# Attention unit of a gated four-layer block: the fourth exponent block joins the partial sum by an accumulating DMA, and the PE sums columns once

## The reference, cut to what matters

```python
def _L1_xattn_ref(q, k, v):
    qh = q.reshape(b * h, d // h, m)          # b 16, h 8 heads, d // h 32, m 512
    kh = k.reshape(b * h, d // h, -1)
    vh = v.reshape(b * h, c // h, -1)
    qk = jnp.einsum('bdm,bdn->bmn', qh, kh) * scale
    sm = jax.nn.softmax(qk, axis=-1)
    ret = jnp.einsum('bmn,bcn->bcm', sm, vh)
    return ret.reshape(b, c, m)
x = x + jnp.tanh(g_xattn[1]) * _L1_xattn_ref(_layernorm(x, axis=-1), ctx_2048, ctx_2048)
```

## Time and profile before

| what | value |
|---|---|
| median of three runs | 1845.89 us (1845.26 to 1846.24) |
| profiled execution | 1844.25 us |
| its span, first to last instruction | 1842.5 us |
| mean granted PE clock | 0.950 of full speed |
| PE busy over the span | 1619.3 us, 88% |
| POOL busy over the span | 850.0 us, 46% |
| attention: first `part_sum` addition to the last | 676.91 us to 1155.94 us |

### The profile page before, as it was taken

One profiled execution on the slowest core, in us unless ns is written; L12 is line 12 of the kernel. 1 busy time (PEld: TensorE's weight loads), 2 busy tenths in 40 slices (PEclk: granted clock), 3 DMA queues, 4 the chain that ended last, 5 costly groups with the idle time before them and its releaser, 6 DMA issues. The chain is left out here.

```text
span 1842.5 us, 24658 instructions
## 1 busy us (share of the span) xinstructions
PE 1619.3 (88%) x6946; PEld 881.0 (48%) x6946; DVE 995.2 (54%) x1724; ACT 660.5 (36%) x1211; POOL 850.0 (46%) x760
## 2 busy tenths in 40 slices
PE   4688888887767279999999999786999999999997
PEld 3566666665533034444444443245444444444443
DVE  6488888888636367777777774275111111111111
ACT  7311111112624536777777777320111111111111
POOL 0344444443304637888888888203333333333332
PEclk9999999998878669999999999887999999999999
DMA  6333333334735785666666661740333333333333
GB/s 184 99 125 125 125 126 127 126 126 108 192 73 213 274 183 133 156 156 155 155 155 155 155 155 53 261 150 24 61 68 68 69 69 69 69 69 69 69 69 46
DMA packets 110369, 223.95 MB, mean 122 GB/s; under 512 B 12256, under 2 KB 12256, under 8 KB 109408
## 3 DMA queue, kind: packets, MB, share of 16 engines
q1 hardware_dynamic: 85696, 169.10, 33.4%
q0 software_dynamic: 15904, 37.23, 11.6%
q10 hardware_dynamic: 8704, 16.78, 2.4%
HBM read 146.71 MB, written 75.84 MB: 121 GB/s over the span
## 5 line engine op out<-in xcount | busy, mean ns | idle before, releaser
L1362 DVE TENSOR_REDUCE low<-pA 128x2 f32<-128x1024 f32 x256 | 307.5, 1224 | 143.3 <-PE pA L1198 132.4
L400 PE MATMUL y<-kv,toep 128*128 128x288 f32 x1280 | 329.2, 413 | 47.7 <-DVEq L63 36.6
L1328 ACT ACTIVATE pt<-pB 128x512 f32<-128x512 f32 x512 | 286.9, 593 | 125.0 <-PE pB L1216 119.2
L400 PEld LDWEIGHTS y<-kv,toep 128*128 128x128 f32 x1280 | 239.3, 191 | 137.6 <-DVEq L63 64.8
L1774 POOL DMA_INDIRECT out_rows<-XN,slots x71 | 112.6, 1587 | 356.7 <-DVE XN L1757 356.7
L1700 PE MATMUL pH<-WF,XN 128*128 x568 | 257.2, 596 | 1.1 <-DVE XN L1748 0.9
L1715 PE MATMUL pY<-WP,XN 128*128 x568 | 255.6, 593 | 0.8 <-ACT XN L1741 0.8
L1216 PE MATMUL pB<-qs,ks 98*128 98x512 f32 x512 | 227.0, 447 | 2.9 <-ACT pt L1328 2.4
L357 POOL TENSOR_TENSOR kv<-kc 128x2048 f32<-128x2048 f32 x32 | 115.2, 3600 | 243.0 <-DMA kc<-in_ctx_conv 177.5
L1198 PE MATMUL pA<-ks,qs 96*128 96x512 f32 x512 | 189.0, 414 | 36.0 <-DMA qs<-q_low 34.4
L1748 DVE COPY XN<-p9T 128x512 f32<-128x512 f32 x71 | 49.1, 692 | 258.4 <-PE p9T L1692 258.4
(11 more groups left out here) (241 smaller groups left out, 1951.7 us busy)
## 6 DMA issues: line engine op xcount, KB each, us to landing
ks<-ctx_high SPq DMA_DIRECT2D x64, 256.0 KB, 4.7
qs<-q_high SPq DMA_DIRECT2D x64, 256.0 KB, 6.2
kc<-in_ctx_conv SPq DMA_DIRECT2D x32, 384.0 KB, 5.8
XN<-in_x SPq DMA_DIRECT2D x16, 512.0 KB, 4.2
ct<-in_ctx SPq DMA_DIRECT2D x16, 512.0 KB, 4.8
toep<-kernel_and_skip SPq DMA_DIRECT2D x32, 256.0 KB, 4.2
ctx_high<-kh ACTq DMA_DIRECT2D x16, 512.0 KB, 5.3
ctx_low<-kl ACTq DMA_DIRECT2D x16, 512.0 KB, 7.0
```

Of the source, the lines that this page charges most:

```text
L400: m = pe.matmul(y[half].rearrange("p (l n) c -> p l n c", l=CB)[:, l, :, 0:PAIRS], toep[u][:, (l - s) * P:(l - s + 1) * P], kv[u][:, half, ...
L1328: act.activation(pt[s][:, h, :], bank(u, n), ACT.Exp, scale=SCALE1).then_inc(s_exp, 1)
L1362: dve.tensor_reduce(ap(low[u % 2], t % CB * NH + t // CB, [[NH, 2], [1, 1]]), pA[n % 2], op=ALU.max, axis=AX.X, negate=True).then_inc(s_re ...
```

## The change

The fourth block of exponents no longer goes to PE for its column sums. POOL issues two transfers from SBUF to SBUF, each adding half of `pt[3]` (128 rows of 4 KB) to the same half of `part_sum`, and PE then sums `part_sum` alone. `part_sum` has two buffers, chosen by the parity of the unit. Each POOL addition now waits for its own half of the exponents. The blocks on PE move: `values` s = 0 to beat 15 of the unit, s = 1, 2, 3 to beats 2, 5, 7 of the next, the one `sums` to its beat 11. The logarithm moves to after the exponent of beat 12, the inverse to after that of beat 14, `scale` to beat 15.

```diff
-        part_sum = sb(st, "part_sum", [P, NH, C])
+        part_sum = [sb(st, f"part_sum{i}", [P, NH, C]) for i in range(2)]
+        s_acc = [sem(f"s_acc6{i}", st) for i in range(2)]
+        def landed(eng, j, i, u):
+            eng.wait_ge(s_acc[u % 2], 32 * (TRIP // 2 * i + u // 2) + 32)
             def body(j, i, u):                     # POOL
-                pool.wait_ge(s_exp, made(j, place(j, 1, NH - 1)))
-                wait(pool, s_sum, 2 * j - 1)
+                mine = part_sum[u % 2]
+                wait(pool, s_sum, j - 1)
                 for n in range(2):
+                    pool.wait_ge(s_exp, made(j, place(j, 1, 2 * n + 1)))
-                    pool.tensor_tensor(part_sum[:, 2 * n:2 * n + 2], pt[0][...], pt[1][...], ALU.add)
+                    pool.tensor_tensor(mine[:, 2 * n:2 * n + 2], pt[0][...], pt[1][...], ALU.add)
...
+                for n in range(2):
+                    pool.wait_ge(s_exp, made(j, place(j, CB - 1, 2 * n + 1)))
+                    pool.sem_inc(s_go, 1)
+                    pool.dma_start(mine[:, 2 * n:2 * n + 2], pt[CB - 1][:, 2 * n:2 * n + 2], accum_op=ALU.add).then_inc(s_acc[u % 2], 16)
                 if exists(j - 1):
                     add_row(j - 1)
...
-            def sums(j, u, last):                  # PE: two calls, beats 5 and 7
+            def sums(j, i, u):                     # PE: one call, beat 11
+                landed(pe, j, i, u)
+                wait(pe, s_att, j)
                 for h in range(NH):
-                    m = pe.matmul(pO[...], ones, rows[:, h, :], start=not last, stop=last)
+                    m = pe.matmul(pO[...], ones, part_sum[u % 2][:, h, :], start=True, stop=True)
             def finish(j, i, u, beat):
                 if beat == 2:
+                    values(j, i, u, 1)
+                if beat == 5:
                     values(j, i, u, 2)
-                if beat == 5:
-                    sums(j, u, False)
                 if beat == 7:
-                    sums(j, u, True)
-                if beat == 10:
                     values(j, i, u, 3)
+                if beat == 11:
+                    sums(j, i, u)
...
-                    if beat == 13:
+                    if beat == 15:
                         values(j, i, u, 0)
-                    if beat == 15:
-                        values(j, i, u, 1)
...
-                    else:                          # ACT, before exponent block 3
-                        wait(act, s_sum, 2 * j)
+                    elif exists(j - 1):
+                        landed(act, *following(j, i, u, -1))
```

More of the change, by code:

```diff
@@ L1162, in body @@
                     halves(j + 1, (u + 1) % TRIP)
-                pool.wait_ge(s_exp, made(j, place(j, 1, NH - 1)))
-                wait(pool, s_sum, 2 * j - 1)
+                mine = part_sum[u % 2]
+                wait(pool, s_sum, j - 1)
                 for n in range(2):
-                    pool.tensor_tensor(part_sum[:, 2 * n:2 * n + 2], pt[0][:, 2 * n:2 * n + 2], pt[1][:, 2 * n:2 * n + 2],
+                    pool.wait_ge(s_exp, made(j, place(j, 1, 2 * n + 1)))
+                    pool.tensor_tensor(mine[:, 2 * n:2 * n + 2], pt[0][:, 2 * n:2 * n + 2], pt[1][:, 2 * n:2 * n + 2],
                                        ALU.add).then_inc(s_add, 1)
                     pool.wait_ge(s_add, 4 * j + n + 1)
-                pool.wait_ge(s_exp, made(j, place(j, 2, NH - 1)))
                 for n in range(2):
-                    pool.tensor_tensor(part_sum[:, 2 * n:2 * n + 2], part_sum[:, 2 * n:2 * n + 2], pt[2][:, 2 * n:2 * n + 2],
+                    pool.wait_ge(s_exp, made(j, place(j, 2, 2 * n + 1)))
+                    pool.tensor_tensor(mine[:, 2 * n:2 * n + 2], mine[:, 2 * n:2 * n + 2], pt[2][:, 2 * n:2 * n + 2],
                                        ALU.add).then_inc(s_add, 1)
                     pool.wait_ge(s_add, 4 * j + n + 3)
+                for n in range(2):
+                    pool.wait_ge(s_exp, made(j, place(j, CB - 1, 2 * n + 1)))
+                    pool.sem_inc(s_go, 1)
+                    pool.dma_start(mine[:, 2 * n:2 * n + 2], pt[CB - 1][:, 2 * n:2 * n + 2], accum_op=ALU.add).then_inc(s_acc[u % 2], 16)
                 if exists(j - 1):
@@ L1228, in values @@
                 m.then_inc(s_av, 1)
-            def sums(j, u, last):
-                if last:
-                    pe.wait_ge(s_exp, made(j, place(j, CB - 1, NH - 1)))
-                else:
-                    pe.wait_ge(s_add, 4 * j + 4)
-                    wait(pe, s_att, j)
-                rows = pt[CB - 1] if last else part_sum
+            def sums(j, i, u):
+                landed(pe, j, i, u)
+                wait(pe, s_att, j)
                 for h in range(NH):
-                    m = pe.matmul(pO[(u + 1) % 2][h * HD1:(h + 1) * HD1, :], ones, rows[:, h, :], start=not last, stop=last)
+                    m = pe.matmul(pO[(u + 1) % 2][h * HD1:(h + 1) * HD1, :], ones, part_sum[u % 2][:, h, :], start=True, stop=True)
                 m.then_inc(s_sum, 1)
@@ L1293, in logarithm @@
             def logarithm(j, u):
-                act.wait_ge(s_sum, 2 * j + 2)
+                act.wait_ge(s_sum, j + 1)
                 wait(act, s_inv, j)
@@ L1336, in body @@
                             keep(j + 1, bank(u, TURN), made(j, TURN))
-                        if NH * s + h == TURN and exists(j - 1):
+                        if NH * s + h == TURN + 2 and exists(j - 1):
                             logarithm(j - 1, u - 1)
-                        if NH * s + h == TURN + 2 and exists(j - 1):
+                        if NH * s + h == TURN + 4 and exists(j - 1):
                             inverse(j - 1)
@@ L1384, in body @@
                         measure(j - 2, (u + 2) % TRIP)
-                    if beat == 13 and exists(j - 1):
+                    if beat == 15 and exists(j - 1):
                         scale(j - 1, u - 1)
```

## The result

The changed kernel takes 1936.31 us (median of 4 runs, 1935.43 to 1937.16) against 1846.07 us for the kernel before on the same chip: ratio 1.0488, 95% interval 1.0469 to 1.0506, so 90 us slower. The prediction said slower, 1903 us with 1846 to 1950 as its range. The sign and the first cause held. The size was short by 33 us, and lies outside the 1877 to 1928 that the prediction gave for its own mechanism. The profile shows why: a late landing and a falling clock took part, which the prediction had counted at nothing and at 2%.

The account below looks back on a forecast made before the run. PE paced the attention before; POOL, with two 1.5 us transfers, would set 17.1 us units. Attention +52.4 and stage end +5.3 give +57.7 on 1844.25, 1902, forecast as 1903 us against the median; range 1846 to 1950.

Parts of the forecast that it names:

- its own mechanism: Attention: POOL as the bound, one transfer costing 1.07 to 1.9 us; 1877 to 1928 us, taken at 1903, chance 67%.
- POOL becomes the bound: Attention unit: two transfers at 1.5 us each on POOL's 14.1 us of work make a unit 17.1 us.
- The rival of a nearly free issue: POOL's two issues: under 0.5 us per transfer, so PE sets the unit; 1822 or 1814 us, chance 14%.
- PE would fall to 14.0 us: PE's attention unit: one sums block fewer takes 1.19 us off 15.18, with DVE and ACT not becoming the bound.
- A late landing costs nothing: PE's wait at `sums`: a late landing costs up to 0.4 us, covered by PE's 3.1 us to spare.
- signs of being wrong: Profile: cheap POOL issues with PE at 100%, `sums` and exponent block 3 waiting for landing, or granted clock under 1.00.
- the engine-bound rival: Transfer engines: adding 4 KB rows takes twice the scatter's time, making units 19.0 us; 1960 us, chance 10%.
- The rival of a falling clock: PE's clock halves because PE idles 3 of 17 us; a unit is 28 us, +400 us, chance 2%.
- The first units: First three attention units: without `add_row` or `refine` in part, 13.4 to 14.8 us of POOL work each, 43.6 together.
- The end of the stage: After the last additions: PE waits 6.3 us for the landing and saves one block, 1.0; +5.3 us.
- The cover for POOL's new wait: POOL's wait for exponent block 3 before issuing: exponents are done 1.7 us before its additions end, so no cost.
- The draw: POOL's issues: with SP's 0.48 us per transfer a unit is 15.06 us; 1846 us in all, chance 7%.

## Why the prediction was right, and where it fell short

*POOL becomes the bound.* Right, and shown twice: against the kernel without transfers, 46 us are lost with two one-column transfers and 92 with four. POOL's floor is 16.76 us against 17.1 forecast. One transfer was taken as 1.5 us with its gap; two are 1.79 us together, with a single gap of 0.65 ahead of them, 2.44 in all and inside its bounds of 2.1 to 3.8. From the last addition to the end of `add_row` are 3.76 us where they were 1.47; that and wider gaps between the additions (0.16 us for 0.08) put the floor 16.76 - 14.1 = 2.65 us above the work that POOL had before, instead of 3.0. The rival of a nearly free issue is out. The Trainium skill (DMA: Bandwidth & Descriptors, Anatomy of one DMA — SWDGE path) calls descriptor generation small; this case's trace does not agree, with a row of 0.89 us of busy POOL for 128 rows.

*PE would fall to 14.0 us.* Wrong, and hidden behind the first point. That step divided PE's order into blocks and matmuls and let neither DVE nor ACT become the bound because each has some 11 us of work in a unit. Both reach PE through two buffers only, so they hold it up over a few beats, though not over the unit. Without transfers the unit is 15.48 us in the new order, 15.13 in the old, 14.5 with half the reductions. The last shows it for DVE; for ACT it is read from PE's waits and no run isolates it. The rivals that ended at 1822 and 1814 us could not have come about at all: the best that this order allowed, with a free fourth block, was 1853.

*A late landing costs nothing.* This is the step that made the forecast 33 us short. It took 4.8 to 7.1 us for the landing; it is 9.8. It let PE's slack pay, 3.1 us; the slack was 16.76 - 15.48 = 1.3. And it gave no price to the half clock that followed many of these waits, but to a fallen clock of the whole stage, at 2%. Of the 37 us between one-column and full transfers (1936.3 - 1899.5), the later loads give back 30 and busy work in the idle stretch 20, so they overlap and do not add up.

*The signs and the range.* Of the signs of being wrong that the prediction listed, two came, `sums` waiting for the landing and a granted clock under 1.00. With one-column transfers the kernel takes 1899.5 us, 3.5 under the forecast, so its own mechanism was priced to within 4 us. That 1936 lies in the stated range is luck: the room up to 1950 was left for the engine-bound rival, which did not come about. In the changed kernel the transfer engines were at 0.79, and they carried 0.89 in units of 15.5 us once POOL was relieved. That rival's price rested on a misread row too: at 1.11 of the engines the window of the earlier trace rows moved 88 KB in its microsecond (88 GB/s), not 256 KB; 1 MB of these additions took 5.2 us, where it had 4.4. The rival of a falling clock, put at 2% because PE kept its clock while busy 35 of 50 us in another stage, was half right: not for the whole stage, but after many of the stalls.

*The first units.* Forecast 43.6 us for three; the casts at 674.26 and 725.45 are 51.2 apart, though POOL had idle time there. The first of them, 17.3 us, is not the landing's doing: without any transfer it is 17.3 as well. In both executions the granted clock was still 0.50 up to 684 us, while it was 1.00 from 674 in the kernel before and from 678 with one-column transfers, where that unit took 14.7. In the other two, 16.6 and 17.3 us, PE waited 1.05 and 1.65 us for the landing; with one column they are 15.5 and 15.6. The other periods are 18.0 on average instead of 17.1, which is 28 x 0.9 = 25 us. With 2.3 us at the end of the stage, below, that is the whole difference between the growth of the span (1935.2 - 1842.5 = 92.7) and the sum that was forecast (57.7): 7.6 + 25 + 2.3 = 34.9. The first addition starts 2.1 us earlier than before (674.84), and what follows the last sums takes 2.2 us longer, which cancels.

*The end of the stage.* Forecast 6.3 us from the last addition to the sums. Measured 1246.48 - 1237.90 = 8.6, with the sums block at half clock, 1.94 us.

*The cover for POOL's new wait* (exponents ready 1.7 us before POOL) held in the short units and not in the long ones: 1.43 us at 954.26, of which 0.65 is the gap that stands there always.

*The draw* was added up wrongly: -6.3 and +4.3 are 2 us less than before, 1844 us and not 1846.

## What to carry to other kernels

Count a transfer that POOL issues as POOL work, however few its bytes, and an adding one at half as much again as a copy (0.89 us against 0.57), and put it against POOL's idle time in one unit before anything else. When an engine that set the pace is relieved, ask over how few steps its neighbours can fall behind: with two buffers, a neighbour at 73% of the unit was already next in line here. A wait on PE is priced also with the matmuls that may follow it at half clock, and loads that can be issued anywhere should not start together with the one transfer that someone waits for.

## What the runs showed of the hardware

An adding transfer of 128 rows within SBUF holds POOL for 0.89 us, a copy for 0.57; a pair of adding ones takes 1.79 us with 4 KB in a row and 1.81 with one column. 1 MB of additions took the 16 engines 5.2 us, 1 MB of copies 2.9. One-column additions still took 5.1 us to land. The POOL instruction behind two adding transfers starts before the second one's row ends (904.25 against 904.86) and shows 1.93 us instead of 1.28. That is no slowdown: it ends at 906.18, and 904.86 + 1.28 is 906.14. Behind copies, without the overlap, it shows 1.29. After PE had stood still for 1.86 us until 913.76 the granted clock went to 0.66 and 0.50, and it stayed at 1.00 after 1.65 us until 714.57. With 64 more blocks on PE and no idle stretch, the kernel ended 20 us sooner.
